# A graph-attention kernel on one Trainium2 core: adjacency tiles loaded as bf16 through GpSimd's queue, four tiles gathered apart

## What is computed

```python
q = x @ Wq.T + bq
k = key @ Wk.T + bk
v = value @ Wv.T + bv
s = (q @ k.T) / 64 * adj
s = where(abs(s) < 1e-5, -1e9, s)
out = layernorm(x + softmax(s) @ v @ Wm.T + bm)
```

## Time and profile before

| | |
|---|---|
| median of 3 runs | 565.24 us (560.36 to 566.16) |
| the profiled execution's own time | 560.05 us |
| its span | 558.2 us |
| mean granted TensorE clock | 0.973 of full |
| HBM and DMA | 160.81 MB moved, mean 288 GB/s |

### The profile page before, as it was taken

How to read it: one execution, slowest core, us unless ns; L and a number is a source line. 1 busy time by engine, 2 the same in 40 slices (tenths; PEclk the granted TensorE clock), 3 DMA queues, 4 the chain that set the end, 5 groups by cost and what they waited for, 6 DMA issues and landing times.

```text
span 558.2 us, 5679 instructions
## 1 busy us (share of the span) xinstructions
PE 510.8 (92%) x1678; PEld 267.3 (48%) x1678; DVE 337.4 (60%) x756; ACT 229.7 (41%) x463; POOL 232.0 (42%) x205
## 2 busy tenths in 40 slices
PE   6999999999389974999999989999999999999983
PEld 3444444444134443556555545555555555555651
DVE  1574678976961047678688888765645543453552
ACT  0233123333123222334552554464373464465473
POOL 3000020008600366466675565655664565466400
PEclk9999999999879996999999999999999999999996
DMA  9999999999999999595899899656547455346422
GB/s 350 423 406 426 426 422 387 384 397 418 408 395 356 340 418 389 175 360 206 320 383 408 318 292 354 217 162 212 164 150 242 105 182 187 99 144 227 114 76 79
DMA packets 43957, 160.81 MB, mean 288 GB/s; under 512 B 9874, under 2 KB 9874, under 8 KB 37778
## 3 DMA queue, kind: packets, MB, share of 16 engines
q1 hardware_dynamic: 20690, 102.21, 47.0%
q0 software_dynamic: 16992, 38.26, 22.3%
q10 hardware_dynamic: 6240, 19.92, 9.0%
HBM read 161.98 MB, written 25.17 MB: 335 GB/s over the span
## 4 chain that ended last, share of the span: by engine, by line
PE 43%; DMA 22%; DVE 19%; SPq 8%; ACT 4%; issue 3%; POOL 0%; ACTq 0%; DVEq 0%; POOLq 0%
DMA big<-adj_tiles 16%; PE bank L496 13%; PE bank L602 11%; PE bank L622 10%; SPq L353 7%; DVE big L898 7%; PE bank L578 5%; DMA table<-key 4%; DMA kv<-table,index 2%; PE bank L612 1%; DVE big L933 1%; DVE slots L931 1%; PE bank L593 1%; DVE big L901 1%; DVE score L1035 1%
## 5 line engine op out<-in xcount | busy, mean ns | idle before, releaser
L392 POOL DMA_INDIRECT kv<-table,index x90 | 100.1, 1112 | 111.5 <-PE bank L622 89.2
L487 PE MATMUL bank<-kv,big 128*128 128x512 f32 x256 | 113.6, 604 | 10.6 <-DMA big<-valueT 10.6
L496 PE MATMUL bank<-big,M 128*128 128x512 f32 x256 | 120.0, 596 | 0.0
L421 POOL DMA_INDIRECT adj_g<-adj_cols,index x96 | 107.8, 1123 | 29.3 <-issue 29.3
L898 DVE TENSOR_TENSOR big<-big 128x2048 bf16<-128x2048 f32 x32 | 73.2, 2288 | 41.3 <-DMA big<-adj_tiles 41.3
L602 PE MATMUL bank<-keyT,qT 128*128 128x384 f32 x256 | 88.9, 490 | 6.2 <-issue 4.9
L622 PE MATMUL bank<-kv,probT 128*128 128x512 f32 x192 | 89.7, 604 | 0.9 <-ACT probT L809 0.6
L487 PEld LDWEIGHTS bank<-kv,big 128*128 128x128 f32 x256 | 49.1, 193 | 72.6 <-issue 61.0
L602 PEld LDWEIGHTS bank<-keyT,qT 128*128 128x128 f32 x256 | 47.6, 190 | 46.7 <-issue 19.1
L496 PEld LDWEIGHTS bank<-big,M 128*128 128x128 f32 x256 | 44.6, 192 | 34.2 <-issue 34.2
L1030 DVE SCALAR_TENSOR_TENSOR score<-bank,c_cols,adjT 128x384 f32<-128x384 f32 x32 | 19.8, 618 | 67.8 <-PE bank L602 66.4
(11 more groups left out here) (99 smaller groups left out, 522.4 us busy)
## 6 DMA issues: line engine op xcount, KB each, us to landing
big<-adj_tiles SPq DMA_DIRECT2D x32, 2048.0 KB, 11.3
big<-valueT ACTq DMA_DIRECT2D x8, 1024.0 KB, 13.4
x_buf<-x SPq DMA_DIRECT2D x32, 256.0 KB, 4.5
table<-key SPq DMA_DIRECT2D x8, 1024.0 KB, 22.8
out<-y_buf SPq DMA_DIRECT2D x32, 256.0 KB, 3.7
big<-xT SPq DMA_DIRECT2D x6, 1024.0 KB, 12.0
table<-qT ACTq DMA_DIRECT2D x4, 1024.0 KB, 20.9
table<-y_buf ACTq DMA_DIRECT2D x4, 1024.0 KB, 28.5
```

Of the source, the lines that this page charges most:

```text
L392: pool.indirect_dma_start(kv[:, b, c, :], None, table, bass.IndirectOffsetOnAxis(index[:, t, c:c + 1], 0), bounds_check=N - 1, oob_is_err= ...
L421: pool.indirect_dma_start(adj_g[:, b, c, :], None, adj_cols, bass.IndirectOffsetOnAxis(index[:, t, CH + c:CH + c + 1], 0),).then_inc(adj_g ...
L487: mm = nc.tensor.matmul(bank[4 + t % 2][:, :], col_buf[nb % 2][:, d, k * P:(k + 1) * P], G[:, d, :], start=(d == 0), stop=(d == DC - 1))
L496: mm = nc.tensor.matmul(ps[:, :], M[:, d, a * P:(a + 1) * P], col_buf[nb % 2][:, d, :], start=(d == 0), stop=(d == DC - 1))
```

## The change

Adjacency tiles are loaded by GpSimd's queue into four bf16 buffers (the transfer converts float32 to bf16, so 2 MB are read and 1 MB is written), each load behind a stated number of finished value units. 18 trees are ahead of the loop, 14 in it (one in each of iterations 0 to 13), and list 2 starts in iteration 6. EARLY becomes 4: keys, adjacency columns and values of four tiles are gathered apart, so that the table is first needed by tile 4. SyncE copies the keys into the table from the 28th finished unit on. V' goes through three slots instead of four. `lists(0)`, `spread_slots(0)` and `lists(1)` move to behind units 13, 19 and 28. `reduce_tile` is the same code on bf16 input; list 1 still stands behind tree 17 in VectorE's order.

```diff
-VS = 4
+VS = 3
-EARLY = 2
+EARLY = 4
+AB = 4
...
-        adj_buf = [big[:, i * 4096:(i + 1) * 4096] for i in range(2)]
+        adj_buf = [big[:, i * 2048:(i + 1) * 2048].bitcast(BF16) for i in range(AB)]
...
-        FIRST = 20
-        LIST_AT = {2: 5, 3: 14}
+        FIRST = 18
+        LIST_AT = {2: 6, 3: 14}
-        V_SLOT = (0, 1, 2, 3, 0, 1, 2, 0)
+        V_SLOT = (0, 1, 2, 0, 1, 2, 0, 1)
...
-            for t in range(4):
-                load_adj(t)
             sp.dma_start(w_left, wq.rearrange("(e p) d -> p e d", p=P)).then_inc(weights_in, 16)
             sp.dma_start(w_right, wk.rearrange("(e p) d -> p e d", p=P)).then_inc(weights_in, 16)
-            for t in range(4, FIRST):
-                load_adj(t)
             for t in range(XB):
                 load_x(t)
+            sp.wait_ge(v_ps, UNITS - DC)
             for nb in range(NB):
                 sp.dma_start(table[nb * 512:(nb + 1) * 512, 0:D], key[nb * 512:(nb + 1) * 512, :]).then_inc(table_in, 16)
-            for t in trees_of(0):
-                load_adj(t)
...
+            def load_adj(t):
+                if t >= AB:
+                    pool.wait_ge(adj_used, t - AB + 1)
+                pool.dma_start(adj_buf[t % AB], adj_tiles[t]).then_inc(adj_in[t % AB], 16)
...
+            pool.wait_ge(weights2_in[DC - 1], 32)
+            for t in range(2):
+                load_adj(t)
             nc.gpsimd.memset(kv_flat[:, 0:kv_half], 0.0).then_inc(kv_zeroed, 1)
+            pool.wait_ge(prep_ps, DC)
+            for t in range(2, AB):
+                load_adj(t)
+            for t, units in ((4, 2), (5, 3), (6, 5), (7, 6), (8, 8)):
+                pool.wait_ge(v_ps, units)
+                load_adj(t)
+            pool.wait_ge(prep_ps, DC + 3)
+            load_adj(9)
             pool.wait_ge(prep_ps, 2 * DC + 3)
+            load_adj(10)
...
+            for t, units in ((11, 10), (12, 13), (13, 16), (14, 18), (15, 21)):
+                pool.wait_ge(v_ps, units)
+                load_adj(t)
             pool.wait_ge(index_ready, 2 * CH)
-            pool.wait_ge(kv_zeroed, 2)
             for t in range(EARLY):
                 gather_keys(t)
                 gather_adj(t)
-            for t in range(EARLY, KV):
-                gather_adj(t)
+            for t, units in ((16, 24), (17, 27)):
+                pool.wait_ge(v_ps, units)
+                load_adj(t)
             pool.wait_ge(spare_sb, KV)
...
             for t in range(EARLY):
                 gather_values(t)
+            for i in range(2):
+                for t in trees_of(i):
+                    load_adj(t)
             pool.wait_ge(table_in, 16 * NB)
-            for t in range(EARLY, T):
-                gather(t)
+            for i in range(1, T - KV + 1):
+                for t in trees_of(i + 1):
+                    load_adj(t)
+                gather(i + KV - 1)
...
-                if t == 12:
+                if t == 13:
                     pe.wait_ge(prep_sb, 2 * DC + 1)
                     lists(0)
-                if t == 17:
+                if t == 19:
                     pe.wait_ge(prep_sb, 2 * DC)
                     spread_slots(0)
-                if t == 25:
+                if t == 28:
                     lists(1)
```

More of the change, by code:

```diff
@@ L110, in build @@
         kv_half = KV // 2 * CH * 2 * D
-        G, w_left, w_right = (kv_flat[:, kv_half + i * 2048:kv_half + (i + 1) * 2048].rearrange("p (e d) -> p e d", e=DC)
-                              for i in range(3))
+        w_left, w_right = (kv_flat[:, kv_half + i * 2048:kv_half + (i + 1) * 2048].rearrange("p (e d) -> p e d", e=DC)
+                           for i in range(2))
         adj_g = sb("adj_g", [P, KV, CH, P])
@@ L125, in build @@
         y_buf = sb("y_buf", [P, YB, D])
-        v_out = [qT[:, 1, :, :], y_buf[:, 0:DC, :], y_buf[:, DC:2 * DC, :], qT[:, 0, :, :]]
+        v_out = [qT[:, 1, :, :], y_buf[:, DC:2 * DC, :], qT[:, 0, :, :]]
+        G = y_buf[:, 0:DC, :]
         v_part = sb("v_part", [P, NB, DC])
@@ L158, in build @@
         bm_in = sem("bm_in")
-        adj_in = [sem(f"adj_in{i}") for i in range(2)]
+        adj_in = [sem(f"adj_in{i}") for i in range(AB)]
         cols_in = [sem(f"cols_in{i}") for i in range(2)]
@@ L286, in trees_of @@
         def trees_of(i):
-            t = FIRST + i - (i > LIST_AT[2])
-            return [t] if i != LIST_AT[2] and t < T else []
+            return [FIRST + i] if FIRST + i < T else []
         def list_step(i):
@@ L324, in load_xT @@
                 sp.dma_start(col_buf[nb % 2], xT[nb]).then_inc(cols_in[nb % 2], 16)
[L326 to L329, removed]
             def load_x(t):
@@ L362, in _ @@
                     load_x(i + XB - 1)
-                for t in trees_of(i + 1):
-                    load_adj(t)
             for t in finish_of(T):
@@ L424, in gather_adj @@
                     ).then_inc(adj_gathered[b], 16)
+            pool.wait_ge(weights2_in[DC - 1], 32)
+            for t in range(2):
+                load_adj(t)
             nc.gpsimd.memset(kv_flat[:, 0:kv_half], 0.0).then_inc(kv_zeroed, 1)
-            pool.wait_ge(prep_ps, 2 * DC + 3)
-            nc.gpsimd.memset(kv_flat[:, kv_half + 2048:2 * kv_half], 0.0).then_inc(kv_zeroed, 1)
+            pool.wait_ge(prep_ps, DC)
[6 more added lines that the diff above has]
+            load_adj(9)
+            pool.wait_ge(prep_ps, 2 * DC + 3)
+            load_adj(10)
+            nc.gpsimd.memset(kv_flat[:, kv_half:2 * kv_half], 0.0).then_inc(kv_zeroed, 1)
+            pool.wait_ge(kv_zeroed, 2)
+            for t, units in ((11, 10), (12, 13), (13, 16), (14, 18), (15, 21)):
+                pool.wait_ge(v_ps, units)
+                load_adj(t)
             pool.wait_ge(index_ready, 2 * CH)
-            pool.wait_ge(kv_zeroed, 2)
             for t in range(EARLY):
@@ L441, in _ @@
                 gather_values(t)
-            nc.gpsimd.memset(kv_flat[:, kv_half:kv_half + 2048], 0.0).then_inc(kv_zeroed, 1)
-            pool.wait_ge(kv_zeroed, 3)
+            for i in range(2):
+                for t in trees_of(i):
+                    load_adj(t)
             pool.wait_ge(table_in, 16 * NB)
-            for t in range(EARLY, T):
-                gather(t)
+            for i in range(1, T - KV + 1):
+                for t in trees_of(i + 1):
+                    load_adj(t)
+                gather(i + KV - 1)
             with overflow(pool) as n:
@@ L768, in copy_q @@
                 if u in (0, DC):
-                    act.wait_ge(v_stored[V_SLOT[3] if u == 0 else V_SLOT[0]], 16 * V_USES[V_SLOT[3] if u == 0 else V_SLOT[0]])
+                    act.wait_ge(v_stored[2 if u == 0 else 0], 16 * V_USES[2 if u == 0 else 0])
                 if nb >= QB:
@@ L894, in reduce_tile @@
             def reduce_tile(t):
-                dve.wait_ge(adj_in[t % 2], 16 * (t // 2 + 1))
+                dve.wait_ge(adj_in[t % AB], 16 * (t // AB + 1))
                 if t >= 1:
                     dve.wait_ge(tree, 3 * t)
-                nc.vector.tensor_tensor(t1, adj_buf[t % 2][:, 0:2048], adj_buf[t % 2][:, 2048:4096], ALU.logical_or
+                nc.vector.tensor_tensor(t1, adj_buf[t % AB][:, 0:2048], adj_buf[t % AB][:, 2048:4096], ALU.logical_or
                                         ).then_inc(adj_used, 1)
@@ L1054, in normalise @@
                 dve.wait_ge(pv_ps, t + 1)
-                if t == 0:
-                    for k in (1, 2):
-                        dve.wait_ge(v_stored[k], 16 * V_USES[k])
+                if t == DC:
+                    dve.wait_ge(v_stored[1], 16 * V_USES[1])
                 if t >= YB:
```

## The result

| | before | after |
|---|---|---|
| median, both on the same chip | 562.8 us (558.92 to 566.16, 4 runs) | 575.35 us (574.9 to 576.93, 4 runs) |
| profiled execution | 560.05 us | 575.53 us |
| its span | 558.2 us | 573.6 us |
| mean granted TensorE clock | 0.973 | 0.956 |

The ratio of after to before is 1.023, with an interval of 1.015 to 1.031: the change makes the kernel slower, by 12.5 us by the medians. The prediction was 567.2 us, within 1% of before, in a range of 552 to 590. The time lies in the range, but the likeliest case, within 5 us of 567, is not what happened. The result lies between it and the first rival (582).

A forecast was written before the change was run, and what follows sets the result against it. Bound: TensorE, busy 92%, plus waits ahead of the loop costing 12.9 and 10.5 us; VectorE paces iterations 6 to 11. Terms +5.6 - 4, about +2 on 560.05, give 562; with the median's 5.2 carried over, 567.2; range 552 to 590.

The forecast's parts named there:

- Value product: Last value units, ahead of the loop: the 10.60 us wait for `valueT` goes, units end at about 159 us, not 171.
- Gathers: GpSimd's queue: 24 gathers start at 122 us and take 33, so the loads of tiles 16 and 17 leave at 155.
- Loads 16 and 17: Two converting adjacency loads behind the gathers: 6.3 us a tile, both landed at 170 us (ends 162 and 185).
- Tree: VectorE's tree 17, behind its load: OR falls from 2.29 to 1.23 us, the tree takes 3.3, done at 173.3.
- List 1 and the sum: VectorE behind tree 17: 11.0 and 0.6 us; L560 starts at 185, 13.8 us later, and TensorE stands 26 us.
- To `keys(0)`: From L560 to the loop: 19.1 us plus 2.3 for the slow start; `keys(0)` at 206.4, 16.1 us later than before.
- The wait at `keys(2)`: TensorE's wait for the table goes, -10.5 us; later loads and gathers are covered by 0 to 20 us, tile 18 least.
- The loop: Steady iterations: a tree with a list step takes 10.94 us instead of 12.0; -4 us in all (ends -6 and 0).
- Late landing: Loads 16 and 17 behind 24 gathers: tile 17 lands at 185 instead of 170, +17 us, 582; chance 0.27.
- Quick loads: Same loads: 24 gathers in 30 us, tile 17 lands at 160 to 162, 9 us less, 558; chance 0.16.
- The whole gain: Ahead of the loop: both waits go, list 1 in time, TensorE never stands; -27 us, 538; chance 0.07.
- Slow conversion or issue: Adjacency loads: above 10 us a tile, the first 16 also push value units and lists; +30 us, 597; chance 0.08.

The follow-up runs named there:

- the first experiment: Kernel after, with tiles 16 and 17 loaded right behind tile 15, ahead of the 24 gathers: 552.02 us, ratio 0.984 to the kernel before.
- The fourth experiment: Kernel after, with GpSimd waiting for the two query-projection weights before loading tiles 2 and on: 565.9 us, ratio 1.007 to the kernel before.

## Where the prediction was right and where it failed

In the order of its steps, with L574 as the check point (forecast 185, measured 202.05):

1. **Value product.** Right that the wait for `valueT` goes. Wrong that the units end at 159: they end at 166.6 (155.79 + 10.82). It cost nothing by itself, but the same delay sits in step 2.

2. **Gathers.** "That is the point on which the forecast rests: two loads stand behind 24 gathers in one queue." This holds; the first experiment shows it. 24 gathers were put at 33 us, and the loads went out 31.6 after the first. One of them took 1.99 us beside a bf16 L912, which started 0.06 us before it; most others take 0.94 to 1.08. By the rule of the Trainium skill weighed in this step (SBUF — State Buffer, Who interferes with whom) it would have been 30 us in all and no such gather; the traces speak for the holding up. Before, the 18 gathers had three that took over 2 us, the 3.04 of the earlier trace rows and these two, and each of the three lies on one of the three L898 of that stretch; together they took some 4.5 us more than three of 0.95:

```profile
125.39 2.17 POOL L402 DMA_INDIRECT kv<-key,index  x1 [0.30 <-issue]
...
138.96 2.25 POOL L421 DMA_INDIRECT adj_g<-adj_cols,index  x1 [0.30 <-issue]
```

After, only one tree's OR fell on the 24, at the cost of a microsecond; "fewer trees run beside them" was right. The time that fails is the start: "say 122" was 132.8, 10.8 us more. 8.1 of them are the wait for `wk` at 52 us with the slow restart behind it (M's first copy at 64.57 against 56.48), the other 2.7 the landing of tile 14, 11.4 us from its issue to its L912. The step had "8 to 12 us later" and then counted less. The wait for `wk` was in no step and no rival: I had the rule about packets in hand and applied it only to who gets the bandwidth at the two late loads, not to who is left without it. The fourth experiment takes 8.3 of the 10.8 away.

3. **Loads 16 and 17.** "Two tiles: 156 + 12.6 + 1.5 = 170" was 187.18. Besides the late issue, the landing took 22.0 us where I had 15: the plain rate beside one other queue was the wrong row. Between 165 and 187 us two other queues are busy:

```profile
q0 software_dynamic: 528, 2.52, 55.2%
q1 hardware_dynamic: 1084, 2.15, 28.4%
q10 hardware_dynamic: 510, 1.77, 19.7%
```

GpSimd's queue has 55% of the engines here, not the 80% of the adjacency queue in the earlier trace rows. Nor are the packets alike in number: SyncE's queue with the key copies got twice as many as each of the others. So the packet rule, by which the prediction kept its 14 us, is not borne out by these rows; why SyncE's queue got more, no run shows. 55.2% of 22 us are 12.1 us of engine time: 10.2 for two tiles at 5.1, the rest for other transfers in that queue, the last gathers probably. With the loads behind twelve gathers, in part ahead of the key copies, the landing took 17.8.

4. **Tree.** L912 takes 1.23 us, as worked out from the two smaller shapes. The group of all 32:

```profile
L912 DVE TENSOR_TENSOR big<-big 128x2048 bf16<-128x2048 bf16 x32 | 39.0, 1217 | 99.7 <-DMA big<-adj_tiles 99.7
```

5. **List 1 and the sum.** From L912 of tree 17 to L574 14.9 us were forecast and 14.87 came. So L574 is late by 10.8 (the indices) - 0.6 (gathers, from the indices to the loads) + 7.0 (the landing) = 17.2 us, which is the whole difference to within rounding, and TensorE stood 35.4 us instead of 26.

6. **To `keys(0)`.** 21.2 us, forecast 21.4. The slow restart was worth 2.1, forecast 2.3. `keys(0)` is 33.0 us later than before, not 16.1.

7. **The wait at `keys(2)`.** Gone, and from `keys(0)` to `scores(2)` it is 11.2 us less than before, forecast 10.5. Tile 18 "has the least" cover: right, its L912 waited 2.18 us. But this cover exists only because VectorE comes late to it in this kernel, at 233.46; in the first experiment it came at 196.87. The step had that a late tile 18 delays "not TensorE's first work"; in four of the experiments a late tree there is TensorE's next wait, of 8.88, 13.82, 10.04 and (with float32) 8.19 us. Where the four tiles were taken apart alone, it ate the whole 10 us.

8. **The loop.** VectorE's period in iterations 7 to 10 is 10.9 to 11.1 us, where it was 12.0 in iterations 7 to 11 (the prediction calls them 6 to 11); from `scores(2)` to the end it is 6.3 us shorter, in place of 4:

```profile
304.32 0.62 DVE L1044 SCALAR_TENSOR_TENSOR score<-bank,c_cols,adjT 128x384 f32<-128x384 f32 x1 [0.21 <-issue]
...
348.20 0.62 DVE L1044 SCALAR_TENSOR_TENSOR score<-bank,c_cols,adjT 128x384 f32<-128x384 f32 x1 [0.20 <-DVE c_cols L992]
```

The sum is +33.0 - 11.2 - 6.3 = +15.5 us by the profiled executions, where the prediction had +16.1 - 10.5 - 4 = +2. The mechanism was right and two of its terms were too small: the time at which the indices are ready (by 10.8) and the landing of the two loads (by 7.0).

The number looks better than the working was. By the profiled executions the sum was 562 and 575.53 was measured, 13.5 us more. The forecast of 567.2 misses the median, 575.35, by only 8.2, because it carried over the 5.2 us by which the median before lay above the profiled execution; after, the median lies 0.2 us below it. That part was luck, and so was some of the rest: the loop and the stretch to `scores(2)` gave 3.0 us more than forecast, against the 16.9 that `keys(0)` was later.

**The rivals.** *Late landing* put tree 17's load at 185 for a loss of 17 us, and it was 187 with 15.5; it is the case that came nearest, though more than half of L574's lateness (10.2 of 17.2 us) lay ahead of the landing. *Quick loads* falls: half the bytes written did not make a transfer quicker, by the two rows of 5.1 us. *The whole gain* fails for the reason given against it, but most of it was not out of reach: with the four loads and the weights moved, the best kernel is 19 us (by the ratio) to 23 us (by the medians) below the kernel before, where this rival had 27. That it has 538.2 us and the rival had 538 is chance, because the rival counted from 565.24. *Slow conversion or issue* falls: 5.1 us of engine time a tile, and an issue takes GpSimd 0.53 to 0.60 us.

What stays open: the third V' slot and the list positions behind other units were not tried singly. In two profiles the last units waited, 5.54 us for ScalarE's copy of a unit with list 1 moved and 7.11 us with the weights first, both hidden by the later wait for VectorE. The wait for `wk` differs between executions of kernels that have the same code up to there, from 2.5 to 7.1 us in the profiles; why it does, no run shows.

## What to carry to other kernels

When a load moves to another engine's queue, follow the order on the issuing engine first: the load leaves behind everything issued there before it, and here the place of two loads was worth some 22 us. Then look at who else uses the DMA engines: a small load that must be early does not share them fairly with long rows of another queue. And when a wait is taken away, find the load it had been hiding: in three of these kernels a tree's late load took back between three tenths and all of what had been gained ahead of it.

## What the runs showed of the hardware that I had not expected

- From 20 to 50 us 702 packets went to each of two queues that both had loads waiting, and a 1 MB weight in packets of 2 KB took 54.8 us beside a queue of adjacency rows, against 12.6 in one queue with them. The Trainium skill (DMA: Bandwidth & Descriptors, Issuing engines are not separate DMA queues) has a second issuing engine save issue time and nothing more. Here it also changed who gets the DMA engines, by 8 us on the path. The numbers are not equal everywhere: from 165 to 187 us they were 528, 1084 and 510.
- A load that converts float32 to bf16 takes the same 5.1 us of the DMA engines for a tile as a plain one. Its use is at the reader: L912 takes 1.23 us instead of 2.29.
- TensorE's clock over the long wait, by windows of 20 us (stretch, its length, busy us and instructions of PE, PEld, DVE, ACT and POOL, granted clock, DMA share, GB/s): 1.00 at work, then 0.50, the lower of its two levels, when it stood all the time:

```profile
140.00:160.00 20.00, 20.00 (x51) 8.82 (x50) 2.02 (x5) 6.37 (x17) 15.43 (x16) 1.00 0.80 273
160.00:180.00 20.00, 6.62 (x15) 2.39 (x13) 0.00 (x0) 2.90 (x7) 5.18 (x7) 0.72 1.03 299
180.00:200.00 20.00, 0.00 (x0) 0.00 (x0) 15.48 (x29) 0.00 (x0) 0.00 (x0) 0.50 1.03 321
200.00:220.00 20.00, 17.95 (x41) 8.21 (x42) 3.31 (x19) 4.10 (x7) 7.21 (x8) 0.85 0.39 126
```

The slow work behind a wait did not grow with its length. L574's group took 5.74 us behind 35.43 us of waiting, 2.1 more than the 3.60 before. The same group took 6.55 behind 23.44, 6.69 behind 16.17, 5.71 behind 15.86 and 6.76 behind only 3.58, but 3.70 behind 3.77. So a short wait can cost 3 us more than it lasts, or nothing.
